# Normalised rows on ScalarE in place of VectorE, in a four-layer transformer kernel on one core

## What is computed

```
def _ln(x, g, b):
    mu = jnp.mean(x, axis=-1, keepdims=True)
    var = jnp.mean(jnp.square(x - mu), axis=-1, keepdims=True)
    return (x - mu) * jax.lax.rsqrt(var + EPS) * g + b
```

## Time and profile before

| | |
|---|---|
| median of 3 runs | 4299.66 us (4295.97 to 4301.73) |
| profiled execution, its own time | 4300.15 us |
| span of its profile | 4298.4 us |
| PE busy | 4069.6 us, 95% |
| DVE busy | 3742.6 us, 87% |
| ACT busy | 2718.3 us, 63% |
| POOL busy | 1863.6 us, 43% |
| mean granted clock of PE | 0.98 |

### The profile page before, as it was taken

One profiled execution on the slowest core, in us unless ns is written; L12 is line 12 of the kernel. 1 busy time (PEld: TensorE's weight loads), 2 busy tenths in 40 slices (PEclk: granted clock), 3 DMA queues, 4 the chain that ended last, 5 costly groups with the idle time before them and its releaser, 6 DMA issues. The chain is left out here.

```text
span 4298.4 us, 106109 instructions
## 1 busy us (share of the span) xinstructions
PE 4069.6 (95%) x36480; PEld 3458.8 (80%) x36480; DVE 3742.6 (87%) x12517; ACT 2718.3 (63%) x7085; POOL 1863.6 (43%) x3089
## 2 busy tenths in 40 slices
PE   4899999999999899999999999998999999999998
PEld 3688888888887678778778888777888888888887
DVE  4899999999998799999999999986888888888886
ACT  2566666667676555555555555554777777777776
POOL 4455545455554234445445455445222232222333
PEclk8999999999999899999999999999999999999999
DMA  4554545454554454544544544534223222222220
GB/s 149 151 153 142 156 142 161 137 155 140 149 152 117 127 169 117 147 138 119 146 139 125 158 125 133 152 109 119 81 61 84 69 75 75 70 82 71 75 72 27
DMA packets 403752, 512.52 MB, mean 119 GB/s; under 512 B 133648, under 2 KB 371216, under 8 KB 381712
## 3 DMA queue, kind: packets, MB, share of 16 engines
q1 hardware_dynamic: 395824, 495.51, 40.1%
q10 hardware_dynamic: 7392, 10.24, 0.7%
HBM read 266.30 MB, written 236.72 MB: 117 GB/s over the span
## 5 line engine op out<-in xcount | busy, mean ns | idle before, releaser
L879 ACT ACTIVATE probs_own<-bank 128x384 f32<-128x384 f32 (+2 forms) x1280 | 648.6, 564 | 286.1 <-DVE bank L1130 250.8
L633 POOL TENSOR_SCALAR veps<-meanvar 128x2 f32<-128x2 f32 x256 | 71.6, 280 | 1015.6 <-DVE meanvar L1031 1013.1
L1263 PE MATMUL bank<-w_ff,ffh 128*128 128x256 f32 x2048 | 490.1, 385 | 1.0
L1263 PE MATMUL bank<-kstack_own,qstack_own 96*128 96x256 bf16 (+2 forms) x3072 | 355.4, 250 | 102.9 <-issue 54.2
L1111 DVE CUSTOM_DVE_ANT_0 bank<-bank,mask_words 128x256 f32<-128x256 f32 x1024 | 398.3, 455 | 50.5 <-PE bank L1263 50.3
L1111 DVE DVE_READ_ACCUMULATOR2_ANT nmf_own<- 128x1 f32 x3072 | 429.1, 140 | 0.0
L1263 PEld LDWEIGHTS bank<-w_ff,ffh 128*128 128x128 f32 x2048 | 372.2, 190 | 65.5 <-issue 14.0
L879 ACT ACTIVATE probs_other<-bank 120x512 f32<-120x512 f32 x512 | 289.6, 603 | 161.3 <-PE bank L1263 161.1
L676 POOL TENSOR_TENSOR xb<-xh,vectors_l 128x256 f32<-128x256 f32 x320 | 229.8, 740 | 344.7 <-DMA out<-xb 202.8
L1263 PEld LDWEIGHTS bank<-kstack_own,qstack_own 96*128 96x128 bf16 x3072 | 242.7, 99 | 166.9 <-issue 95.3
L944 ACT ACTIVATE probs_other<-bank,negmax 128x120 f32<-128x120 f32 x1024 | 355.8, 380 | 31.0 <-DVE negmax L1229 31.0
(11 more groups left out here) (200 smaller groups left out, 12668.0 us busy)
## 6 DMA issues: line engine op xcount, KB each, us to landing
qstack_own<-q_parts SPq DMA_DIRECT2D x96, 768.0 KB, 5.7
kstack_own<-k_parts SPq DMA_DIRECT2D x64, 768.0 KB, 6.4
qstack_other<-q_parts SPq DMA_DIRECT2D x64, 768.0 KB, 6.1
q_parts<-q_parts_own SPq DMA_DIRECT2D x96, 384.0 KB, 3.5
k_parts<-k_parts_own SPq DMA_DIRECT2D x64, 384.0 KB, 2.5
q_parts<-q_parts_own SPq DMA_DIRECT2D x96, 256.0 KB, 3.0
q_parts<-other_parts SPq DMA_DIRECT2D x64, 384.0 KB, 3.0
other_words<-k_parts SPq DMA_DIRECT2D x64, 360.0 KB, 3.6
```

Source lines behind the costliest of these rows:

```text
L633: nc.gpsimd.tensor_scalar(veps[key][:, :], meanvar[key][:, :, 1], r["norms"][key]["eps"], None, ALU.add).then_inc(veps_ready.sem, 1)
L879: nc.scalar.activation(probs[key][0:rows, j % a.slots, 0:n], bank_of(u)[0:rows, 0:n], ACT.Exp, scale=a.scale).then_inc(a_done.sem, 1)
L1263: return nc.tensor.matmul(out, lhsT, rhs, start=first, stop=True, skip_group_check=True)
```

## The change

The step `norm` of DVE goes. A step `xhat` of ACT comes, at the same time of the list at which DVE had `norm` (so it stands before ACT's own `norm`), for all eight norms. It makes xh = x * rstd + shift with two activations of 128 x 256. The shift, -mean * rstd, is a new tile `shift_of` of 128 x 2 for each norm; POOL's `stats` makes it with two more instructions, and waits for each before the next. All who waited for DVE's `norm` (PE's transposes, POOL's `xb`, the loads of x) wait for `xhat`. DVE's `stats` and two mask steps of the third pass get waits for work of the element before. The lists, of which one line of each pass stands here for all, are otherwise as they were, and so is the plan of the banks.

```
@@ LISTS, l0
-            weights_hi.own_qkv.0/0.10000 norm.0.0/0.61022 split_hi_k.own.0/0.78032 split_hi_q.own.0/0.81685
+            weights_hi.own_qkv.0/0.10000 xhat.0.0/0.56288 norm.0.0/0.61022 split_hi_k.own.0/0.78032 split_hi_q.own.0/0.81685
...
-            stats.0.0/0.18229 norm.0.0/0.56288 split_rest_k.own.0/0.80509 split_rest_q.own.0/0.85177 masks.l1.0/1.20000
+            stats.0.0/0.18229 split_rest_k.own.0/0.80509 split_rest_q.own.0/0.85177 masks.l1.0/1.20000
...
@@ GpSimd, stats
                 nc.gpsimd.tensor_scalar(veps[key][:, :], meanvar[key][:, :, 1], r["norms"][key]["eps"], None,
                                         ALU.add).then_inc(veps_ready.sem, 1)
-                if w.new(xhat_ready, ("norm", key, 0), 1):
-                    g.wait_ge(xhat_ready.sem, w.value(xhat_ready, ("norm", key, 0), 1))
+                if w.new(xhat_ready, ("xhat", key, 0), 1):
+                    g.wait_ge(xhat_ready.sem, w.value(xhat_ready, ("xhat", key, 0), 1))
+                nc.gpsimd.tensor_scalar(shift_of[key][:, :], meanvar[key][:, :, 0], -1.0, None, ALU.mult).then_inc(minus_ready.sem, 1)
                 if w.new(veps_ready, u.tag):
                     g.wait_ge(veps_ready.sem, w.value(veps_ready, u.tag))
-                nc.gpsimd.tensor_tensor(rstd[key][:, :], veps[key][:, :], half[:, :], ALU.pow).then_inc(rstd_ready.sem, 1)
+                nc.gpsimd.tensor_tensor(rstd[key][:, :], veps[key][:, :], half[:, :], ALU.pow).then_inc(pow_ready.sem, 1)
+                if w.new(minus_ready, u.tag):
+                    g.wait_ge(minus_ready.sem, w.value(minus_ready, u.tag))
+                settle(g)
+                if w.new(pow_ready, u.tag):
+                    g.wait_ge(pow_ready.sem, w.value(pow_ready, u.tag))
+                nc.gpsimd.tensor_tensor(shift_of[key][:, :], shift_of[key][:, :], rstd[key][:, :], ALU.mult).then_inc(rstd_ready.sem, 1)
...
@@ ScalarE
+            elif kind == "xhat":
+                src = r["norms"][key]["src"]
+                x = x_in[:, u.element % 2] if src == "x_in" else xn[src]
+                if w.new(rstd_ready, ("stats", key, 0)):
+                    act_e.wait_ge(rstd_ready.sem, w.value(rstd_ready, ("stats", key, 0)))
...
+                for t in range(QT):
+                    ins = affine(xh[key][:, t, :], x[:, t, :], rstd[key][:, t:t + 1], shift_of[key][:, t:t + 1])
+                ins.then_inc(xhat_ready.sem, 1)
...
@@ VectorE, stats
+                if w.new(minus_ready, u.tag, 1):
+                    settle(dve)
+                    dve.wait_ge(minus_ready.sem, w.value(minus_ready, u.tag, 1))
...
-            elif kind == "norm":
...
-                for t in range(QT):
-                    ins = v.tensor_scalar(xh[key][:, t, :], x[:, t, :], meanvar[key][:, t, 0:1], rstd[key][:, t:t + 1],
-                                          ALU.subtract, ALU.mult)
-                ins.then_inc(xhat_ready.sem, 1)
...
@@ TensorE
-                    if w.new(xhat_ready, u.tag):
-                        pe.wait_ge(xhat_ready.sem, w.value(xhat_ready, u.tag))
+                    if w.new(xhat_ready, ("xhat", key, 0)):
+                        pe.wait_ge(xhat_ready.sem, w.value(xhat_ready, ("xhat", key, 0)))
```

More of the change, by code:

```diff
@@ L97 @@
[L97 to L101, removed]
+            stats.0.0/0.18229 split_rest_k.own.0/0.80509 split_rest_q.own.0/0.85177 masks.l1.0/1.20000 scores_max.own.2/1.26811
@@ L102 @@
+            project_out.own.0/2.20999 stats.1.0/2.22725 split_rest_q.other.0/2.46842 project_v.other.0/2.68514
             scores_max.other.2/2.82528 scores_max.other.3/2.83852 scores_max.other.7/2.87195 scores_max.other.1/2.88519
@@ L179 @@
             negate_t.other.0/3.42259 probs_v.other.1/3.82693 probs_v.other.0/3.84105 heads_rec.other.0/3.85777
-            heads_back.other.0/3.95252 project_out.other.0/4.13340 stats.2.0/4.15441 norm.2.0/4.21679 ff_out.ff.0/5.00791
-            stats.3.0/5.77789 norm.3.0/5.86374
+            heads_back.other.0/3.95252 project_out.other.0/4.13340 stats.2.0/4.15441 ff_out.ff.0/5.00791 stats.3.0/5.77789
         """,
@@ L403, in bank_of @@
         return banks[holds[tag or u.tag, u.element][0]]
-    x_in, ct, moments, meanvar, veps, rstd, xh, ht, xb, xn = (t[n] for n in (
-        "x_in", "ct", "moments", "meanvar", "veps", "rstd", "xh", "ht", "xb", "xn"))
+    x_in, ct, moments, meanvar, veps, rstd, shift_of, xh, ht, xb, xn = (t[n] for n in (
+        "x_in", "ct", "moments", "meanvar", "veps", "rstd", "shift_of", "xh", "ht", "xb", "xn"))
     qstack, kstack, q_parts, remains, ot_raw, v_aug, probs, nmf, nm_parts, nm_t, rec, ctx_q, ctx_t = (t[n] for n in (
@@ L421, in run @@
     moments_ready = counts("moments_ready", "DVE", ("stats",))
-    xhat_ready = counts("xhat_ready", "DVE", ("norm",))
+    xhat_ready = counts("xhat_ready", "ACT", ("xhat",))
     hi_ready = counts("hi_ready", "ACT", ("split_hi_q", "split_hi_k"))
@@ L445, in run @@
     veps_ready = counts("veps_ready", "POOL", ("stats",))
+    minus_ready = counts("minus_ready", "POOL", ("stats",))
+    pow_ready = counts("pow_ready", "POOL", ("stats",))
     rstd_ready = counts("rstd_ready", "POOL", ("stats",))
@@ L806, in _ @@
                 if first and kind == "norm":
-                    reuse(act_e, w, u, xhat_ready, [("norm", "2", 0)], u.element - 1)
+                    reuse(act_e, w, u, xhat_ready, [("xhat", "2", 0)], u.element - 1)
                 for count, tag in ahead["ht_users"][key](a_full, d_full):
@@ L1012, in _ @@
                 dve.wait_ge(rest_loaded, n_rest)
-            if kind in ("stats", "norm"):
+            if kind == "stats":
                 src, made = r["norms"][key]["src"], r["norms"][key]["made"]
@@ L1064, in _ @@
                         dve.wait_ge(a_full.sem, w.value(a_full, tag, 1))
+                else:
+                    tag = latest(w, masked_by_dve, "mask_scores", "own", r["atts"]["own"].exp_count(), 1)
+                    if u.element % NB and w.new(masked_by_dve, tag, 1):
+                        settle(dve)
+                        dve.wait_ge(masked_by_dve.sem, w.value(masked_by_dve, tag, 1))
                 rows = bank_of(u)[0:S2, 0:T // 2].bitcast(BF16)
@@ L1629, in build @@
     each(norms, "veps", [P, QT])
+    each(norms, "shift_of", [P, QT])
     each(norms, "rstd", [P, QT])
```

96 lines of the change are left out of this document (52 added, 44 removed).

## The result

| | before | after |
|---|---|---|
| median of 18 runs each | 4296.12 us (4289.85 to 4305.64) | 4311.94 us (4303.53 to 4323.89) |
| ratio to before | | 1.0036 (95%: 1.0027 to 1.0044) |
| span of the profiled execution | 4298.4 us | 4322.2 us |
| busy: PE, DVE, ACT, POOL | 4069.6, 3742.6, 2718.3, 1863.6 us | 4066.1, 3582.2, 2967.9, 1973.7 us |

The change costs 15.8 us, 0.36%. The profiled execution after is the longest of its 18, so its span overstates that by some 8 us (23.8 us between the two spans, 15.8 between the medians). VectorE is busy for 160 us less, ScalarE for 250 more, GpSimd for 110 more, and PE is busy as long as before: no gain in it. The removed pairs had 221 us, so some of it came back in other instructions of VectorE: the product for probs_other alone has 192.2 us in place of 163.6 (772 ns each for 660).

The account below looks back on a forecast made before the run. Bound: PE in the third pass, PE plus one DMA-chain wait in the first two. Profiled 4300.15 + 8.0 (SP delay) + 1.6 (first and last element) - 3 (pass changes) = 4306.75, adjusted to 4306.3 us; range 4280 to 4332.

Parts of the forecast that it names:

- First pass, 0 on ScalarE: First norm of the first pass: ScalarE's shift mostly hidden, as it waits for PE before each turned copy; cost 0.
- Second pass, +8 through SP: Norm 3: GpSimd's products delay SP's burst by 0.5 us, half reaching PE through the k stack; +8.0 us.
- C: Rival, slower: GpSimd's products cost more and pass one to one through SP to the k stack; +27, 4326 us; chance 0.20.
- Second pass, norm 1: ScalarE's rows 0.12 us late for PE's transposes, absorbed by the later k stack wait; 0, at most 10 us.
- VectorE's relief: 221.4 us taken from VectorE gain 0 in steady state; bounds 0 and 107 us, PE's idle time in two passes.
- Rival B: Faster: VectorE holds PE in passes one and two, so relief delivers the burst earlier; -53, 4247 us; chance 0.20.
- Third pass, 0: Norm 1 has 0.31 us of cover, norm 3 stands where ScalarE waits for PE; cost 0, period stays 41.41 us.
- Price of a pair on ScalarE: Each norm's two activations take 1.02 us and put ScalarE's queue back by 0.92 us, 236 us in all.
- The two products: GpSimd's two added 128x2 instructions for each norm: 0.25 us each, 0.5 together; bounds 0.2 and 1.4 us.

Follow-up runs that it names:

- only_l0_key0: Kernel before, with only the first norm of the first pass made by ScalarE, with its two GpSimd products; 4323.56 us, 1.0043 of before.
- pool_l1: Kernel before, with GpSimd's two products added in the second pass only, their shift unread, all rows still by VectorE; 4317.62 us, 1.0038 of before.
- l1_only: Kernel before, with all three norms of the second pass made by ScalarE, with GpSimd's products; 4298.60 us, 0.9995 of before.
- l1_k3: Kernel before, with only norm 3 of the second pass made by ScalarE, with its GpSimd products; 4309.73 us, 1.0020 of before.
- l1_k1: Kernel before, with only norm 1 of the second pass made by ScalarE, with its GpSimd products; 4320.15 us, 1.0036 of before.
- l0_early: Changed kernel, with ScalarE making the first norm's rows of the first pass 6 us earlier; 4312.53 us, 1.0016 of before.
- l0_back: Changed kernel, with the first pass put back as before (rows by VectorE, no products there); 4304.48 us, 0.9999 of before.
- l1_k2: Kernel before, with only norm 2 of the second pass made by ScalarE, with its GpSimd products; 4293.42 us, 0.9978 of before.

## Why the prediction was right, and where not

The time, 15.8 us over before, is inside the range and on the side that I gave the largest chance by a little. But the forecast of 6.6 us over its median had two wrong steps in it, which in part made up for each other: the loss is in a pass where the sum has 0, and the pass that has +8 in it gave about -2. That the time fell inside the range is in this sense luck.

- **First pass, 0 on ScalarE: this step failed.** I costed xhat.0 by ScalarE's idle share of the pass. The place had 0.28 us of waiting in front of the turned copy (686.14 in before), and the pair shifts by 0.99. It measured +16 to +21 us (0.5 us a period against the reference, 0.67 against before; 19 us in the time of only_l0_key0, 1.0043). I had looked for a PE step that waits for ScalarE, and not for what GpSimd does after a late copy and whom that meets.
- **Second pass, +8 through SP: right as far as SP, wrong behind it.** SP's wait for other_parts grew by 0.40 us where I had put 0.45. PE's wait for the stack did not follow. The products can cost 17 us (pool_l1, 1.0038), by their meeting with VectorE's pair xh_ff, but only where that pair is still there: in the changed kernel it is gone, and the second pass as a whole gained 2 us (l1_only). C had the engine, and neither the place nor the size (its middle was +27).
- **Second pass, norm 2: left out.** I treated norms 1 and 3 and not this one. It makes PE wait 0.9 us (20.2 us in 23), which the k stack's shorter wait pays back, and it brought the only gain of the change, through the clock, of which the prediction says nothing.
- **Second pass, norm 1: 0.12 us late, and absorbed.** PE was 0.4 us late there, in l1_k1 as in l1_only, and had 0.26 us of it back 2 us later; the rest stays. So the cover was there for the larger part only. What makes l1_k1 1.0036 is in the main the pair xh_ff behind it and the clock.
- **VectorE's relief is worth nothing in the loop: held.** l1_k3 shows it most plainly: the 0.99 us became a wait for PE of 0.83 us in each period. 160 us less of VectorE gave no time. Rival B is out.
- **Third pass, 0: held**, 41.41 us to the hundredth, no wait of PE.
- **Price of a pair on ScalarE: held**, 0.99 us of the queue and 1.12 long, for 0.92 and 1.02. The two products: 0.34 us in the first pass and 0.44 at norm 3 of the second, for 0.5.

Put together: the first norm of the first pass costs some 18 us, and the second pass comes out at -2 (l1_only). Its parts do not add up: norm 1 alone is +16, norm 3 alone +9, norm 2 alone -10. By the second table that is for two reasons: with norm 2 the clock stays at full behind the wait, which is worth 0.4 to 0.6 us a period and outweighs what norm 1 costs; and with norm 3 on ScalarE there is no pair xh_ff on VectorE for GpSimd to meet. Open are the 9 us of l1_k3, the 7 us by which l0_early is slower than l0_back, why some overlaps with GpSimd cost VectorE time and others none, and the ramps: the first statistics of norm 1 behind 300 us came at 332.4 us in l1_only and at 339.6 in l1_k2, which have the same first pass.

## What to carry to other kernels

An engine's idle share says nothing about one place of a fixed order: before moving work there, follow every later instruction of that queue, and what these release, down to the engine that has no slack, and look which SBUF work of VectorE and GpSimd will newly lie side by side. In a schedule that tight, shifts of half a microsecond have the price of whole instructions. And where PE has one long wait in a period, look at the granted clock behind it: here two waits with the same sum cost less than one.

## What was not expected of the hardware

Eight useless copies on ScalarE made the kernel 6 us faster, because PE's wait of about 1.9 us in each period became two, and the granted clock then stayed nearly always at full: 15.4 us lost in 1100 before (10.3 in another profile of the same pass), 1.7 with the copies, and 0.9807 to 0.9828 in the mean clock of all executions. And instructions of VectorE can grow when a GpSimd instruction lies beside them, in steps: 0.33 to 0.75 us for the first of two tensor_scalar of 128x256, 0.42 to 0.73 for the first of two products. It depends on where the starts fall: the second of those tensor_scalar took 0.75 in both cases. The Trainium skill (Perfetto Trace Analysis, "Optimizing Scalar/DVE Operations") says that GpSimd and VectorE share an SBUF read port. The traces agree with it in that these instructions grew only beside GpSimd; no run here isolates the port. It was such an overlap, and not the work taken from VectorE, that made the loss of the first pass.
